# Row maxima of attention: a lookahead of one and a half slots at the opening, two from slot 4 on

## What is computed

```python
x = x + xattn0(layernorm(x), ctx, ctx, mask)      # 8 x 512 x 256, 16 heads
x = x + ternary_ffn(layernorm(x))
x = x + xattn1(layernorm(x), ctx, ctx)            # causal
x = x + gated_ffn(layernorm(x))

# xattn, for each sequence and head
scores = q @ k.T / sqrt(16)                       # 512 x 512, masked
attn = softmax(scores)                            # exp(score - row maximum) / row sum
out = attn @ v
```

## Time and profile before

| | us |
|---|---|
| median of 3 executions | 1446.47 (1446.24 to 1446.83) |
| profiled execution, its own time | 1445.1 |
| span of the profile | 1443.4 |
| opening of attention: first reduction of maxima | 215.0 |
| first exponent product (slot 0) | 233.6 |
| first product of slots 1 and 2 | 246.7, 259.2 |

### The profile page before, as it was taken

The page is one execution under the profiler, slowest core; times in us unless marked ns, Lnnn a source line. Parts: engine busy times, 40 slices in busy tenths (PEclk is TensorE's granted clock), DMA queues, the critical chain, the costliest instruction groups (busy, mean ns, idle before and its releaser), DMA issues. The chain is left out here.

```text
span 1443.4 us, 21219 instructions
## 1 busy us (share of the span) xinstructions
PE 1312.4 (91%) x7367; PEld 646.0 (45%) x7367; DVE 950.9 (66%) x1647; ACT 849.2 (59%) x1489; POOL 422.9 (29%) x639
## 2 busy tenths in 40 slices
PE   7999979999999999999999988999995999960598
PEld 4555532333433434334455534554543444420487
DVE  5444429888788787886666688867753335997532
ACT  3545424767677686777665655665563446859432
POOL 0000000033344443444564432333330002549200
PEclk9999997999999999999999999999997999985699
DMA  8677676323242432423424542333110001416132
GB/s 297 243 265 268 240 207 146 103 87 102 68 125 79 131 114 72 120 84 111 119 77 134 161 137 77 93 113 98 57 31 15 0 0 44 175 49 256 44 102 87
DMA packets 87914, 170.73 MB, mean 118 GB/s; under 512 B 14585, under 2 KB 49156, under 8 KB 86276
## 3 DMA queue, kind: packets, MB, share of 16 engines
q1 hardware_dynamic: 87038, 167.70, 37.0%
q10 hardware_dynamic: 774, 1.72, 0.6%
HBM read 108.27 MB, written 60.31 MB: 117 GB/s over the span
## 5 line engine op out<-in xcount | busy, mean ns | idle before, releaser
L1224 DVE TENSOR_REDUCE b_neg_max<-b_score 128x1 f32<-128x512 f32 (+3 forms) x864 | 540.5, 662 | 199.5 <-PE b_score L784 108.1
L1004 ACT ACTIVATE b_probs<-b_exp 128x512 f32<-128x512 f32 (+1 forms) x864 | 463.4, 582 | 291.5 <-PE b_exp L806 290.6
L781 PE MATMUL b_score<-b_k_stack,b_q_stack 97*128 97x512 bf16 (+3 forms) x1024 | 354.6, 350 | 15.2 <-DVE b_neg_max L1224 14.2
L806 PE MATMUL b_exp<-b_q_stack,b_k_stack 100*128 100x512 bf16 (+3 forms) x1024 | 344.7, 342 | 5.5 <-ACT b_probs L1004 4.7
L827 PE MATMUL b_av<-b_probs,b_values 128*17 128x512 f32 (+3 forms) x2048 | 228.6, 518 | 3.7 <-POOL b_probs L1102 3.4
L781 PEld LDWEIGHTS b_score<-b_k_stack,b_q_stack 97*128 97x128 bf16 x1024 | 99.8, 97 | 250.9 <-DVE b_neg_max L1224 142.8
L1110 POOL CAST b_max_parts<-b_neg_max 128x16 bf16<-128x16 f32 x64 | 12.6, 196 | 488.3 <-DVE b_neg_max L1224 488.0
L806 PEld LDWEIGHTS b_exp<-b_q_stack,b_k_stack 100*128 100x128 bf16 x1024 | 100.2, 98 | 80.9 <-ACT b_probs L1004 22.9
L1102 POOL TENSOR_SCALAR_AFFINE_SELECT b_probs<-b_probs 128x512 f32<-128x512 f32 x96 | 61.5, 641 | 182.7 <-ACT b_probs L1004 182.4
L784 PE MATMUL b_score<-diag_qk,minus_big 128*128 128x128 bf16 x512 | 112.7, 220 | 0.0
L1768 PE MATMUL f_down<-f_w_downT,f_tmp 128*128 128x256 f32 x384 | 85.8, 387 | 4.6 <-DVE f_tmp L1445 4.6
(11 more groups left out here) (215 smaller groups left out, 1771.2 us busy)
## 6 DMA issues: line engine op xcount, KB each, us to landing
b_q_stack<-s_q SPq DMA_DIRECT2D x384, 64.0 KB
s_k<-a_part_k SPq DMA_DIRECT2D x48, 256.0 KB, 5.5
b_k_stack<-s_k SPq DMA_DIRECT2D x60, 192.0 KB
s_up<-f_up SPq DMA_DIRECT2D x6, 1536.0 KB, 5.1
s_va<-a_va SPq DMA_DIRECT2D x16, 544.0 KB, 5.0
b_values<-s_va SPq DMA_DIRECT2D x16, 544.0 KB, 4.4
a_mask_q<-mask_in SPq DMA_DIRECT2D x8, 1024.0 KB, 7.4
out_dram<-normed SPq DMA_DIRECT2D x16, 512.0 KB, 3.0
```

Of the source, the lines that this page charges most:

```text
L781: mm = pe.matmul(o, q, KS[half][0:R_MAX, h, 0:w], start=True, stop=causal or not general)
L806: mm = pe.matmul(o, k, QS[half][0:NSTACK, h, q0:T], start=True, stop=not masked)
L1004: nc.scalar.activation(probs[kc][:, h0:h0 + m, q0:T], exp_bank[n % RINGS][:, 0:m * w].rearrange("p (h n) -> p h n", h=m), ACT.Exp).then_in ...
L1224: nc.vector.tensor_reduce(neg_max[u][:, qt, h0:h0 + m], score_bank[n % RINGS][:, 0:m * w].rearrange("p (h n) -> p h n", h=m), AX.X, ALU.ma ...
```

## The change

The two slots of lookahead are cut to one and a half at the start, and restored by slot 4:

- A table `MAXIMA[t, s]` says which products of maxima stand in which step. In slot -1, steps 8 to 15 have none (`HELD` = 8). In slots 0 to 3, steps 7 and 15 have two. All other steps have one, as before. From slot 4 on the table is what it was.
- The turn of the maxima stands at step 3 in slot -1, at 11 in slot 0, at 9 in slot 1, at 7 in slot 2, and at 5 in all others.
- PE, DVE and ACT all follow the table. The fill numbers of the two rings are counted in the new order. No instruction is added or removed: PE has as many rows as before.

```diff
@@ -590,7 +590,8 @@
         ROWS_SET = 16 * 2
         NLOADS = 10
         SLOTS = range(-2, LAST + 10)
-        TURN_MAX, TURN_OUT = 5, 10
+        TURN_OUT = 10
+        HELD = 8
 
         def there(t):
             return 0 <= t <= LAST
@@ -611,20 +612,37 @@
             n = [f for f, (tile, h, m) in enumerate(fills) if tile == s // 4 and h <= s % 4 < h + m][0]
             return n, s % 4 - fills[n][1], fills[n][2]
 
+        def maxima_at():
+
+            left = [(u, q) for u in range(LAST + 1) for q in range(STEPS)][::-1]
+            held = HELD // 2
+            for t in SLOTS:
+                for s in range(STEPS):
+                    count = 1
+                    if t == -1 and s >= STEPS - HELD:
+                        count = 0
+                    if 0 <= t < held and s % 8 == 7:
+                        count = 2
+                    yield (t, s), [left.pop() for _ in range(min(count, len(left)))]
+
+        def turn_max_at(t):
+            return {-1: 3, 0: 11, 1: 9, 2: 7}.get(t, 5)
+
+        MAXIMA = dict(maxima_at())
         score_fill, exp_fill = {}, {}
         for t in SLOTS:
             for s in range(STEPS):
-                if there(t + 2):
-                    f, place, m = fill_of(MAX_FILLS, t + 2, s)
+                for u, q in MAXIMA[t, s]:
+                    f, place, m = fill_of(MAX_FILLS, u, q)
                     if place == 0:
-                        score_fill["max", t + 2, f] = len(score_fill)
+                        score_fill["max", u, f] = len(score_fill)
                 if s == TURN_OUT and there(t - 1):
                     score_fill["out", t - 1] = len(score_fill)
                 if there(t):
                     f, place, m = fill_of(EXP_FILLS, t, s)
                     if place == 0:
                         exp_fill["exp", t, f] = len(exp_fill)
-                if s == TURN_MAX and there(t + 1):
+                if s == turn_max_at(t) and there(t + 1):
                     exp_fill["max", t + 1] = len(exp_fill)
 
         def maxima_through(t):
@@ -923,15 +941,15 @@
                     l, b, j = behind(t)
                     e = of_before(t)
                     for s in range(STEPS):
-                        if there(t + 2):
-                            maxima(t + 2, s)
+                        for u, q in MAXIMA[t, s]:
+                            maxima(u, q)
                         if there(t):
                             exponents(t, s)
                         if s == 3 and there(t - 1):
                             weigh(t - 1, TT - 1)
                         elif s % 4 == 3 and s > 3 and there(t):
                             weigh(t, s // 4 - 1)
-                        if s == TURN_MAX and there(t + 1):
+                        if s == turn_max_at(t) and there(t + 1):
                             turn_max(t + 1)
                         if s == TURN_OUT and there(t - 1):
                             turn_out(t - 1)
@@ -1212,16 +1230,16 @@
             def slot(t):
                 l, b, j = behind(t)
                 for s in range(STEPS):
-                    if there(t + 2):
-                        u, qt = t % 2, s // 4
-                        if s == 0 and t >= 0:
-                            dve.wait_ge(max_split, t + 1)
-                        f, place, m = fill_of(MAX_FILLS, t + 2, s)
+                    for u, q in MAXIMA[t, s]:
+                        qt = q // 4
+                        if q == 0 and u >= 2:
+                            dve.wait_ge(max_split, u - 1)
+                        f, place, m = fill_of(MAX_FILLS, u, q)
                         if place == m - 1:
-                            n = score_fill["max", t + 2, f]
+                            n = score_fill["max", u, f]
                             dve.wait_ge(score_full, n + 1)
-                            h0, w = s % 4 - place, widths[layer_of(t + 2)][qt]
-                            nc.vector.tensor_reduce(neg_max[u][:, qt, h0:h0 + m], score_bank[n % RINGS][:, 0:m * w].rearrange("p (h n) -> p h n", h=m),
+                            h0, w = q % 4 - place, widths[layer_of(u)][qt]
+                            nc.vector.tensor_reduce(neg_max[u % 2][:, qt, h0:h0 + m], score_bank[n % RINGS][:, 0:m * w].rearrange("p (h n) -> p h n", h=m),
                                                     AX.X, ALU.max, negate=True).then_inc(score_read, 1)
                     if s == TURN_OUT and there(t - 1):
                         v, g = (t - 1) % 2, (t - 1) % G
```

## The result

The changed kernel takes 1450.93 us (median of 14 executions, 1445.67 to 1455.35), the kernel before beside it 1447.79 us (14 executions, 1444.40 to 1450.14). The ratio is 1.0022, 95% interval 1.0012 to 1.0032: 3.1 us slower, a little over the 2.9 us that I had said can be told from no change. A second set of ten executions gave the same ratio. I had forecast +1.1 us, 1447.6 us, with a range of 1444.2 to 1449.9; the measured 1450.93 lies above it. Of the 3.3 us between forecast and time, 1.3 are no fault of the terms: the kernel before itself took 1447.79 here, where the forecast had counted from 1446.47. The other 2.0 are the sum's.

What follows compares the result with a forecast made beforehand. PE, busy for 91% of the span, was taken to bound the kernel. Terms -3.1 + 0 - 0.9 + 3.3 + 0.4 + 1.4 = +1.1 us on the 1446.47 median gave 1447.6 us, range 1444.2 to 1449.9.

Steps and rivals of the forecast that it cites:

- A: Start of slot 0: first exponent product comes at 230.5, not 233.61, -3.1 us (bounds -3.6 and -1.4).
- Rival 3: Three small DMAs take 2.9 us, not 1.9, from third issue to landing; +3.1 us, 1449.6 us, chance 0.12.
- B: PE's clock in slot 0: the low stretch moves along with the first exponent product, 0 us, 0.7 either way.
- F: Start of slot 2: maxima of group 2 issued late by SP, PE waits +1.4 us (0.4 to 2.5).
- C: Turns of maxima in slots 0 to 2 cost less at their new steps, together -0.9 us (bounds -1.2 and 0).
- D: Eight steps with two products of maxima, slots 0 to 3: six cost 0.52 each, in all +3.3 us (1.5 to 4.2).
- Rival 1: Double steps nearly free at 0.22 us each and landings quick; -1.9 us, 1444.6 us, chance 0.23.
- E: Start of slot 1: PE waits for the maxima of group 1, turned later, +0.4 us (0 to 1.4).
- rival 2: Before slot 2 the small rows queue behind the masks, a 2.5 us wait; sum +2.2, 1448.7 us, chance 0.17.
- The slower case: Outcome for the whole kernel: slower by more than the 0.2% (2.9 us) that can be told, chance 0.12.

Runs made afterwards that it cites:

- e4: Changed kernel plus 13 products that nobody reads, keeping PE busy before the first exponent product of slot 2; 1449.12 us, ratio 1.0014.
- e3: Kernel before with full lookahead, only the turns of maxima moved (steps 11, 9, 7 in slots 0 to 2); 1451.65 us, ratio 1.0035.
- e1: Changed kernel with values and masks of sequence 1 issued behind the maxima of group 2; 1446.63 us, ratio 1.0002.
- e5: The changed kernel itself run once more; 1450.73 us against 1446.81, ratio 1.0022.
- e7: Kernel before with turns at steps 11, 9, 7 of slots 0 to 2, masks and values behind the maxima of group 2; 1446.03 us, ratio 0.9994.
- e8: Changed kernel with only the masks moved behind the maxima of group 2, values staying ahead; 1446.19 us, ratio 0.9993.
- e6: Changed kernel with 6 products held back, not 8, turns at steps 3, 9, 7, 5, masks and values behind group 2's maxima; 1446.53 us, ratio 0.9996.
- e9: Kernel before with the turn of maxima at step 7 in every slot, not 5; 1452.13 us against 1447.92, ratio 1.0049.

## Why the prediction was wrong, point by point

**A was right.** Predicted -3.1, measured -3.34 in every run with the early turn. The exponent product ended a wait for the DMA, as I had said, and landing took 1.7 us where I had set 1.9. Rival 3 is out with it, though its 1449.6 us is nearest to the measured time. Its number came close for a cause that is not there.

**B was the step that failed most.** I counted the low clock at the start only, moved along at no cost, and wrote under F that from slot 4 on everything is only shifted. I never asked what a wait of 1.4 us or more would do to the clock. It fell at slot 2, and 6.5 us of slot 2 at 1.2 GHz cost 2.7 us (15.74 against 13.00, and e4). For the start, the clock rose 3.2 us after the first exponent product in e3, 3.4 in e4, 5.4 to 5.7 before and in e1, e5, e7 and e8, 6.3 after and 6.7 in e6. Between e4 and the changed kernel, with the same code in slot 0, 2.9 us later made the slot 1.10 longer: 0.38 per us, where I had set 0.3. Between e3 and e7, again with one code in slot 0, 2.2 us made 1.08. The spread is 1.1 us in all for the same code, within the 0.7 either way that I had set.

**C was about right.** Predicted 0.34 for each of slots 1 and 2; e7 shows 0.32 at step 9 and 0.53 at step 7. For slot 0 no run parts the turn from the clock.

**D was right in kind and 0.06 too high.** A double costs 0.46: slot 3, where I had one of the two free, is 0.46 above 12.54 in e1, and slot 2, with two and the turn at step 7, is 13.00 against 12.01 in e7, 0.5 each. From the timeline of the changed kernel, steps 4 to 7 of slot 1, a group with a double and no turn:

```profile
250.04 0.39 PE L799 MATMUL b_score<-b_k_stack,b_q_stack 97*128 97x512 bf16 x1
...
250.46 3.08 DVE L1242 TENSOR_REDUCE b_neg_max<-b_score 128x1 f32<-128x512 f32 x5 [0.51 <-PE b_score L799]
...
252.34 1.05 PE L845 MATMUL b_av<-b_probs,b_values 128*17 128x512 f32 x8
253.33 0.39 PE L799 MATMUL b_score<-b_k_stack,b_q_stack 97*128 97x512 bf16 x1
```

The group takes 3.29 in place of 2.83, with five reductions, and nothing piles up behind it. Rival 1 (0.22 each) is refuted. The double at step 7 of slot 3 cost nothing, as I had said: with it, steps 4 to 7 take 3.58 in e1, as before.

**E was right.** The exponent product of slot 1 starts 0.40 after the product of maxima ahead of it (247.02 and 247.42) and not 0.23 (246.68 and 246.91 before): a wait of 0.2 in place of 0.4.

**F was mis-sized.** The mechanism is the one I named, SP handing its lateness on and the masks ahead of the rows, and rival 2 was the case that happened. I took the middle of 0.4 and 2.5; it was 2.9 and 2.4. SP's issue came 12.72 after that for group 1 (I had 13.6). The rows landed 5.2 after their third issue behind the masks, 1.7 with nothing ahead. In the changed kernel they were there 0.8 after the masks, in e3 0.1 before them. By the rule of the Trainium skill (DMA: Bandwidth & Descriptors, Queues, rings and completion order), that descriptors of one row are consumed in ring order on each engine, the wait had to be the upper end, and the traces of e1, e3 and e8 agree with it: 0, 2.65 and 0 us of wait with nothing, all and half of the large transfers ahead. The rule says when the small packets are reached, and that is 1.9 of the 3.5 us that the landing took longer in the changed kernel. The 1.4 behind the last packet are measured and not explained.

**The sum.** Without F and the clock my terms make -0.3; e1, which has neither, shows -1.09 on the way. With them it should have been -0.3 + 2.9 + 2.7 = +5.3, and the trace shows +5.06. So F (1.5 too low) and the clock (2.7, put at nothing) make 4.2 us of error on the way, and the other terms together were 0.8 too high. A forecast of +1.1 that missed the medians by only 2.0 owes that in part to these opposite errors, and to executions that were milder than the profiled ones. The 3.1 us of the medians are under the 5.06 and 4.27 of the profiles for the reason left open under e5. The range has a slip of its own: rival 1 less 0.7 is 1443.9 and not 1444.2. The slower case had 0.12, all of it for the landing; the case that came true had 0.17 and no price for the clock.

## What to carry to other kernels

When a step is moved later, follow the queue that issues its DMA to the next step of the same kind. Lateness is handed on there, and a small transfer that somebody waits for does not belong behind a megabyte that nobody wants yet. Price a wait of PE by its length and by what the clock does after it: here 2.9 us of wait cost 5.6. And compare two traces from an event that both share, slot by slot; the spans of these two differed by twice what the change had done.

## What the runs showed that I had not expected

- PE's clock fell to 0.50 in waits of 2.4 to 2.9 us (after, e5, e3), before the wait was over, and needed some 7 us to come back (263 to 270). Waits of 0.5, 0.6 and 1.2 us (e3 at slot 1, e9 at slot 2, the kernels with the early turn at slot 0, where it was low already) gave nothing to see.
- The same code in slot 0 took 13.29 to 14.39 us, by when the clock rose. Behind attention another 2 us between executions went with the clock, in code that the change does not touch.
- A transpose of maxima behind a `weigh` starts 0.12 us earlier than a product of maxima there (e7), so that the turn at step 7 costs 0.22 in all and not 0.41. In slots with side work the same place costs 0.2 more than step 5 (e9).
